# The first five pairs of sequences in turns of their own, and the last sum on TensorE, in an attention and mixture-of-experts kernel

## The reference, cut to what matters

```python
B, S, D = 16, 256, 128          # sequences, tokens, width; float32
qkv = x @ W_qkv + b_qkv         # q, k, v = split
attn = softmax(q @ k.T / sqrt(D))
x = layernorm(x + (attn @ v) @ W_out + b_out)
h = x + layer_norm(x, ln1_g, ln1_b) @ attn_w.T
t = layer_norm(h, ln2_g, ln2_b)
top_vals, top_idx = top_k(t @ gate_w.T, 2)       # 2 of 8 experts a token
rw = softmax(top_vals)
out = sum over experts e: comb[:, e] * (silu(t @ gate_proj[e].T) * (t @ up_proj[e].T)) @ down_proj[e].T
x = layernorm(h + out)          # INTER = 512
```

## Time and profile before

| | |
|---|---|
| median of 3 runs | 402.53 us (399.04 to 403.39) |
| profiled execution | 403.65 us |
| its span, first to last instruction | 401.8 us |
| PE busy | 312.1 us, 78% |
| DVE busy | 271.3 us, 68% |
| ACT busy | 241.3 us, 60% |
| POOL busy | 202.1 us, 50% |
| mean granted clock of PE | 0.878 |

### The profile page before, as it was taken

One profiled execution on the slowest core, in us unless ns is written; L12 is line 12 of the kernel. 1 busy time (PEld: TensorE's weight loads), 2 busy tenths in 40 slices (PEclk: granted clock), 3 DMA queues, 4 the chain that ended last, 5 costly groups with the idle time before them and its releaser, 6 DMA issues.

```text
span 401.8 us, 8647 instructions
## 1 busy us (share of the span) xinstructions
PE 312.1 (78%) x1972; PEld 267.2 (66%) x1972; DVE 271.3 (68%) x1079; ACT 241.3 (60%) x559; POOL 202.1 (50%) x251
## 2 busy tenths in 40 slices
PE   5645767776899999999999989989999999960000
PEld 4533556564778788888878878778898989850000
DVE  3353465667688688696878887877676766626990
ACT  3243543444668766866777677668777787731551
POOL 0001015565635585475568668588444442336980
PEclk9665575969899999999999999999999999995555
DMA  8234281201231131121112111223211111006851
GB/s 268 87 111 130 81 291 44 62 30 48 67 113 36 41 88 43 34 69 48 42 47 63 49 54 56 56 87 104 62 48 46 41 45 37 14 12 198 233 158 39
DMA packets 31967, 31.96 MB, mean 80 GB/s; under 512 B 4769, under 2 KB 27557, under 8 KB 31920
## 3 DMA queue, kind: packets, MB, share of 16 engines
q1 hardware_dynamic: 23248, 20.78, 18.3%
q0 software_dynamic: 4320, 8.53, 6.5%
q10 hardware_dynamic: 4352, 2.10, 1.7%
HBM read 20.16 MB, written 11.68 MB: 79 GB/s over the span
## 4 chain that ended last, share of the span: by engine, by line
PE 61%; DVE 13%; issue 11%; POOL 6%; ACT 5%; DMA 2%; ACTq 0%; SPq 0%; POOLq 0%; DVEq 0%
PE bank L514 15%; PE bank L467 7%; PE bank L469 7%; PE bank L468 7%; PE bank L500 7%; POOL expert_rows L1115 4%; PE bank L424 4%; PE bank L408 3%; PE bank L386 2%; PE bank L522 2%; PE bank L387 2%; PE bank L415 2%; PE bank L400 2%; DVE xs L1083 2%; DVE hid L1010 1%
## 5 line engine op out<-in xcount | busy, mean ns | idle before, releaser
L1124 POOL DMA_INDIRECT moe_rows<-ysb,xrow x71 | 70.6, 994 | 93.1 <-ACT ysb L661 85.8
L514 PE MATMUL bank<-wd,hidT 128*128 x568 | 76.4, 278 | 4.9 <-ACT t L668 4.1
L514 PEld LDWEIGHTS bank<-wd,hidT 128*128 128x128 f32 x568 | 69.0, 192 | 7.7 <-issue 7.6
L1115 POOL DMA_INDIRECT expert_rows<-rows,place x64 | 62.3, 974 | 22.4 <-issue 16.2
L467 PE MATMUL bank<-w_hi,t_hi 128*128 x142 | 62.6, 441 | 4.4 <-DVE hid L1010 4.3
L469 PE MATMUL bank<-w_hi,t_lo 128*128 x142 | 56.2, 396 | 0.0
L468 PE MATMUL bank<-w_lo,t_hi 128*128 x142 | 55.9, 394 | 0.0
L674 ACT ACTIVATE th<-bank 128x512 f32<-128x512 f32 x71 | 42.5, 599 | 14.3 <-PE bank L469 14.3
L1010 DVE SCALAR_TENSOR_TENSOR hid<-th,bank 128x512 f32<-128x512 f32 x71 | 48.3, 680 | 3.6 <-ACT th L674 3.4
L1014 DVE TENSOR_TENSOR hid<-hid,bank 128x512 f32<-128x512 f32 x71 | 48.8, 687 | 2.4
L687 ACT ACTIVATE hidT<-bank 128x512 f32<-128x512 f32 x71 | 42.5, 599 | 10.8 <-PE bank L500 10.8
(11 more groups left out here) (153 smaller groups left out, 599.6 us busy)
## 6 DMA issues: line engine op xcount, KB each, us to landing
xrow<-expert_rows SPq DMA_DIRECT2D x71, 66.0 KB, 1.9
w_raw<-weights SPq DMA_DIRECT2D x16, 256.0 KB, 2.7
w_raw<-moe_rows SPq DMA_DIRECT2D x16, 256.0 KB, 3.6
xT<-xt SPq DMA_DIRECT2D x8, 256.0 KB, 3.3
wd<-weights SPq DMA_DIRECT2D x4, 512.0 KB, 6.5
out<-xs ACTq DMA_DIRECT2D x16, 128.0 KB, 3.1
xs<-x SPq DMA_DIRECT2D x3, 512.0 KB, 5.0
moe_rows<-ysb,xrow POOLq DMA_INDIRECT x71, 2.3
```

Of the source, the lines that this page charges most:

```text
L514: last = mm(ps_y, hidT[i % 2][:, c * P:(c + 1) * P], wd[:, bass.ds(w + c * P, P)], start=(c == 0), stop=(c == NC - 1))
L1115: G.indirect_dma_start(out=expert_rows[:, :], out_offset=bass.IndirectOffsetOnAxis(ap=place[:, i, k:k + 1], axis=0), in_=rows[:, i, k, :], ...
L1124: G.indirect_dma_start(out=moe_rows[:, :], out_offset=bass.IndirectOffsetOnAxis(ap=xrow[i % XR][:, C_DST:C_DST + 1].bitcast(I32), axis=0), ...
```

## The change

The first five pairs (`FILL`) no longer go by the step counter. They go in five turns, and a turn n holds both sequences of pair n side by side: on two sets of banks (1, 3, 5 and 0, 2, 4, by `side(b)`) and two buffers each of `qT`, `kT` and `probT`. A turn also holds the later places of the pairs before it. The step counter goes on from `STEADY` = 40 as before for pairs 5 to 7 and the tail of pairs 2 to 4, with pairs four steps later (`- CHUNKS // 2` in `at`) and tiles seven steps later (`TILE_FROM` 42 for 35). In `finish`, DVE's and POOL's additions are replaced by three products with the identity on PE, which add up in PSUM over all 8 banks (`ps_z`). The w_lo pieces are made by POOL, 5, 7 and 4 of them in turns 0, 1 and 2, and their loads are issued by SP as early as the buffers allow. Scores and context no longer share a bank; values and context do.

```diff
@@ orders @@
-TILE_FROM = 35
+FILL = 5
+STEADY = CHUNKS * FILL
+TILE_FROM = STEADY + 2
+        PIECES = [(0, 5), (5, 12), (12, 16), (16, 16), (16, 16)]
         def at(q, r):
-            g, left = divmod(q - r, CHUNKS)
+            g, left = divmod(q - r - CHUNKS // 2, CHUNKS)
@@ banks @@
+        side = lambda b: 1 if b % 2 and b < 2 * FILL else 0
+        in_qp, in_s, in_vo = [banks[1], banks[0]], [banks[3], banks[2]], [banks[5], banks[4]]
+        in_a = lambda b: in_nr if b % 2 else banks[6] if b // 2 < FILL - 2 else banks[5]
+        ps_z = lambda b: banks[b % 8][:, 0:NT * D].rearrange("p (t d) -> p t d", t=NT)
@@ PE @@
             def qk(b):
-                if b >= 1:
-                    pe.wait_ge(sm["pT_sb"], b)
+                if b >= 2:
+                    pe.wait_ge(sm["pT_sb"], b - 1 if b < 2 * FILL else b)
             def values(b):
-                if b >= 1:
-                    pe.wait_ge(sm["v_sb"], b)
+                if b >= 2:
+                    pe.wait_ge(sm["y_done"], NT * (b - 1 if b < 2 * FILL else b))
             def scores(b):
-                if b >= 1:
-                    pe.wait_ge(sm["y_done"], NT * b)
+                if b >= 2:
+                    pe.wait_ge(sm["prob_done"], NT * (b - 1 if b < 2 * FILL else b))
+            for n in range(1, FILL):
+                qk(2 * n)
+                qk(2 * n + 1)
+                if n >= 3:
+                    rank(n - 3)
+                if n >= 2:
+                    turn_n1(n - 2)
+                scores(2 * n)
+                scores(2 * n + 1)
+                if n >= 2:
+                    attn_w(2 * (n - 2))
+                    attn_w(2 * (n - 2) + 1)
+                context(2 * n - 2)
+                context(2 * n - 1)
+                turn_prob(2 * n)
+                turn_prob(2 * n + 1)
+                values(2 * n)
+                values(2 * n + 1)
+            for b in range(B):
+                if b >= 8:
+                    pe.wait_ge(sm["o_done"], NT * (b - 7))
+                pe.wait_ge(y_in[b % RING], turn(b))
+                mm(ps_z(b), ident, xs[:, b, :, :], start=True, stop=False)
+                mm(ps_z(b), ident, yin[b % RING][:, :, 0, :], start=False, stop=False)
+                mm(ps_z(b), ident, yin[b % RING][:, :, 1, :], start=False, stop=True).then_inc(sm["z_done"], 1)
@@ ACT, a turn: what is new against the places of a pair @@
+                query_key(2 * n)
+                query_key(2 * n + 1)
+                ...
+                for i in range(third[0], third[1]):
+                    cast(i)
+                softmax(2 * n)
+                softmax(2 * n + 1)
+                ...
+                for j in range(GT if n < FILL - 1 else NT):
+                    x1(n - 1, j)
@@ DVE @@
-                i = piece(q)
-                if i is not None:
-                    dve.wait_ge(sm["whi_done"], i + 1)
-                    V.tensor_tensor(w_lo[:, :, cs], w_raw[i % NWR][:, :, :], w_hi[:, :, cs].bitcast(F32),
-                                    ALU.subtract).then_inc(sm["wlo_done"], 1)
             def finish(s, live):
                 if live(0):
-                    dve.wait_ge(sm["z0_done"], s + 1)
-                    V.tensor_tensor(xs[:, s, :, :], xs[:, s, :, :], yin[s % RING][:, :, 1, :], ALU.add
-                                    ).then_inc(sm["z_done"], 1)
                     dve.wait_ge(sm["z_done"], s + 1)
-                        V.bn_stats(st3[:, t, :], xs[:, s, t, :]).then_inc(sm["st3_done"], 1)
+                        V.bn_stats(st3[:, t, :], ps_z(s)[:, t, :]).then_inc(sm["st3_done"], 1)
@@ POOL @@
+            def split(i):
+                pool.wait_ge(sm["whi_done"], i + 1)
+                G.tensor_tensor(w_lo[:, :, cs], w_raw[i % NWR][:, :, :], w_hi[:, :, cs].bitcast(F32),
+                                ALU.subtract).then_inc(sm["wlo_done"], 1)
+            for n in range(1, FILL):
+                lo, hi = PIECES[n]
+                for i in range(lo, lo + (hi - lo) * 2 // 3):
+                    split(i)
+                if n >= 3:
+                    send_rows(n - 3, (0, 1, 2, 3))
+                if n >= 2:
+                    second_root(n - 2)
+                first_root(n - 1)
+                for i in range(lo + (hi - lo) * 2 // 3, hi):
+                    split(i)
+                if n >= 3:
+                    send_rows(n - 3, (4, 5, 6, 7))
             def finish(s, live):
-                    G.tensor_tensor(xs[:, s, :, :], xs[:, s, :, :], yin[s % RING][:, :, 0, :], ALU.add
-                                    ).then_inc(sm["z0_done"], 1)
```

More of the change, by code:

```diff
@@ L275, in turn, with second @@
             return per * (i // n + 1)
[L278 to L282, removed]
+        PIECES = [(0, 5), (5, 12), (12, 16), (16, 16), (16, 16)]
         def at(q, r):
-            g, left = divmod(q - r, CHUNKS)
+            g, left = divmod(q - r - CHUNKS // 2, CHUNKS)
             return g if left == 0 and 0 <= g < GROUPS else None
+        def second(q, r):
+            g = at(q, r)
+            return g if g is not None and g >= FILL else None
         def tile(q, stage):
@@ L544, in front @@
                     context(2 * g)
+                g = second(q, 4)
+                if g is not None:
                     qk(2 * g + 1)
@@ L1054, in late @@
                     plan_tiles(g)
[L1055 to L1066 removed]
+            largest(0)
+            largest(1)
             dve.wait_ge(sm["dst_in"], 16)
@@ L1074, in _ @@
                           ).then_inc(sm["fill_ready"], 2)
-            for q in range(6, ALL):
+            dve.wait_ge(sm["gate_ps"], 1)
+            V.tensor_copy(wa[:, D + E:D + 2 * E], banks[6][:, D:D + E]).then_inc(sm["wa_ready"], 1)
+            for n in range(1, FILL):
+                if n >= 3:
+                    places(n - 3)
+                largest(2 * n)
+                largest(2 * n + 1)
+                if n >= 2:
+                    hidden(2 * (n - 2))
+                    hidden(2 * (n - 2) + 1)
+                    second_variance(n - 2)
+                residual(2 * n - 2)
+                residual(2 * n - 1)
+                variances(n - 1)
+                if n >= 2:
+                    logits(n - 2)
+                    choose(n - 2)
+                x1_scale(n - 1)
+                if n == FILL - 1:
+                    plan_tiles(1)
+            places(FILL - 3)
+            for q in range(STEADY, ALL):
                 early(q)
@@ new lines, in send_rows @@
+            def send_rows(g, which):
+                if which[0] == 0:
+                    pool.wait_ge(sm["dest_ready"], 1)
+                    pool.wait_ge(sm["c_shift_done"], g + 1)
+                    pool.wait_ge(sm["cr_done"], g + 1)
+                    pool.wait_ge(sm["dup_done"], g + 1)
+                    pool.wait_ge(sm["place_done"], g + 1)
+                    pool.wait_ge(sm["wts_done"], 2 * g + 2)
+                for j in which:
+                    send(g, GT * g + j // TOPK, j % TOPK)
```

270 lines of the change are left out of this document (155 added, 115 removed).

## The result

| | before | after |
|---|---|---|
| median | 402.62 us (399.04 to 403.39, 4 runs) | 390.43 us (390.14 to 390.5, 4 runs) |
| profiled execution, its span | 403.65, 401.8 us | 390.5, 388.7 us |
| first tile's tanh | 110.1 us | 100.38 us |
| first to last tile's tanh | 242.95 us | 240.76 us |
| last tanh to the end of the span | 48.75 us | 47.56 us |

The ratio is 0.9713, 95% interval 0.9655 to 0.9771: faster by 2.9%, 12 us, where 28 were forecast. By the last three lines of the table, which split the spans of the two traces, the tile part gave 2.2 us (forecast 3.5) and the last part 1.2 (1.5). The first part gave 9.7 where 23 were forecast. That is 13.1 us in all, and of the 14.9 that are missing all but 1.6 lie before the first tile's tanh.

A forecast was written before the change was run, and what follows sets the result against it. Before the first tile a chain through four engines, one sequence in flight, was taken as the bound; after it, PE bounds the tiles. 403.65 - 23 - 3.5 - 1.5 = 375.7, given as 375 us; range 366 to 391.

The forecast's parts named there:

- term 1: First part, up to the first tile's tanh: 87 us instead of 110.1, 23 us earlier.
- Turn 2, "15": Second full turn, scores to scores: a 13.3 us loop plus about 2 us for half at the lower clock.
- The way to the first tile, "24": Turn 4's scores to first tanh: last send 17 us in, 2.4 to landing, load 2, remaining steps 3.
- at 1.27 it hides: First part: w_lo pieces on POOL, 1.27 us each, 16 of them 20 us over three turns, cost no time.
- The rival made of it: Turns 1 and 2: 11 POOL pieces each stop a DVE step for 1 us; 386 us, chance 0.06.
- Term 2: Tile part, first to last tanh: attention is 3 tiles further at the first tile; 3.5 us less.
- Term 3: Last part: sums move to PE, two cold sequences, then 1.4 us each; 1.5 us less.
- 1: First part: the turns stay at 1.2 GHz, first tanh at 98, 11 later; 386 us, chance 0.11.
- rival 2: Last part: PE never warms because a load is late each time; 391 us, chance 0.07.
- 5: First part: POOL's subtraction is dear, over 4.4 us a piece, so slower than before; chance 0.03.
- 3: Turns 1 and 2: POOL's pieces block DVE's steps, 1 us each; 386 us, chance 0.06.
- rival 4: First part: waits in order chain the turns at 20 us, so the fill gains little; 390 us, chance 0.07.

The follow-up runs named there:

- e1: Changed kernel, but POOL's last third of a turn's w_lo pieces waits until DVE's short operations are done; 410.55 us, ratio to before 0.9423.
- e3: Changed kernel, but ACT makes the next turn's qT and kT and the gap's exponential ahead of x1; 414.33 us, ratio to before 0.9493.
- e2: Changed kernel with the w_lo pieces back on DVE, in three groups a turn; 419.14 us, ratio to before 0.9618.
- e9: Changed kernel with powers before most pieces, late pieces waiting, ACT reordered, token-row products before the last part's first load, two pieces moved to turn 2; 403.64 us.
- e6: Changed kernel, but in turn 4 POOL sends all of pair 1's rows ahead of the two powers; 419.23 us, ratio to before 0.9539.
- e7: Changed kernel, but the last part's token-row products of the first eight sequences precede the first wait for a load; 415.36 us, ratio to before 0.9446.
- after_third: The changed kernel, unedited, run again beside the third set of experiments; 421.47 us, ratio to before 0.9624.

## Why the prediction was half right

**The step that failed** is term 1, the length of the turns and of the way to the first tile. It put at nothing the waits behind other work in the in-order lists of POOL, ACT and PE, and it said that POOL's pieces hide. The runs showed DVE's short operations standing still beside the pieces (e1), `turn_n1` standing behind the plan's `base` (e3), and contexts and query products ahead of the gate (read from the trace): turns of 17.0 and 19.5 us for 12 and 15, and 29.6 us to the first tile for 24.

**Direction and order of the terms: right.** The first part is where the time came from, and the chain of one sequence at a time was what bounded it.

**Term 1: wrong by 13.4 us**, first tanh at 100.38 for 87. In its steps:
- *Turn 0, "21":* 18.45, 2.5 us better.
- *Turn 1, "12":* 17.0. The step summed up what ACT has to do and held POOL to fit since its pieces' total is small. In its list pieces 7 and 8, which wait for casts, stand ahead of the power: 3.2 us, read from the trace. And DVE's short operations stood still beside the pieces behind it: 3.3 us, which e1 shows. The two make 6.5 where 5.0 are too much, so the first is not worth its full 3.2; no kernel took this wait away alone. In e1, where it stands, the turn is 1.8 us over the forecast, and in e2 and e9, where both are gone, it is 12.9 and 11.8 us.
- *Turn 2, "15":* 19.5. Of the 4.5 us too much, 2.1 are the same standstill (e1: 2.7 us for the turn), and some 2.2 are `turn_n1` behind `base` (e3: 3.5 us for the turn, clock included). The step had counted "the next qT and kT, 0.75" behind x1 and had not asked what PE does ahead of the scores.
- *Turn 3, "15":* 15.8. Here `base` cost 1.6 (e3), and other parts of the turn were shorter than counted.
- *The way to the first tile, "24":* 29.6. The 17 us to the last send were right (16.6), landing and load were 2 us too short, and "tn, transpose, t, split and the gate product, 3" had left out that contexts and query products stand ahead of the gate on PE. This part was not tried by itself: e6 changed what stands before it, and gained 1.0 us there.

In e9, which takes the causes in the turns away together and moves two pieces as well, the turns have the forecast's lengths or less. So the lengths of the turns as PE's, DVE's and ACT's work sets them were about right, and what was wrong is that nothing was counted for waits in order on POOL and ACT. With some luck: the forecast had half of a turn at the lower clock, and e9's turns had 0.90 to 0.97 granted.

**The weight pieces: price right, "at 1.27 it hides" wrong.** They took 1.264 us at the median. They hid in POOL's time, not in the time of those behind and beside them. The rule quoted from the Trainium skill, "SBUF — State Buffer" (Who interferes with whom), described what the trace then showed: `sd`, `lift` and `ratio` have two inputs in SBUF and ended with POOL's piece, while the row maximum, which reads a PSUM bank, took the same 0.69 us beside pieces (at 19.62, 20.48 and 37.56) as without one (39.27). The rival made of it, 11 us, was twice too dear, as five operations were caught and not eleven; but as a part of the sum, 5.4 us, it would have been the largest single correction inside the turns. I gave it 0.06 and the forecast itself nothing of it.

**Term 2: nearly right**, 2.2 us for 3.5. The pace of the tiles without attention was unchanged.

**Term 3: nearly right**, 1.2 for 1.5, by its own steps: two sequences at the lower clock, then 1.42 us each with their waits for loads where 1.4 was said. It left out that PE stands idle for 5.96 us ahead of them, and that is where e7 found 3.7 us.

**Rivals.** 1 and 2 fell: the granted clock was 0.76 to 0.93 in the turns and 1.00 in the last part from 359 us on. 5 fell with the price. 3 and 4 each held in part and at once: waits in order on ACT and POOL made turn 2 19.5 us, near rival 4's 20, but turns 1 and 3 not. The sum came out at rival 4's 390 without being its case. The stated range, 366 to 391, holds 390.43 by luck: its upper end is the price of rival 2, which did not happen. Treating the rivals as other worlds, each with its small chance, hid that parts of two of them were the likeliest case.

## What to carry to other kernels

A step's length is not the sum of one engine's work nor the largest such sum: for each wait that closes a loop, list what stands ahead of the awaited instruction on its own engine, and what that in turn waits for; three such lists (POOL's power, ACT's exponential, PE's gate) hold 8 to 10 of the 13 us here by the traces, of which ACT's alone was tried by itself. Work moved to an idle engine should be put behind what others wait for on that engine, and away from short operations of DVE with two SBUF inputs, or it costs more than it did where it was. And what makes the first tile earlier must not make the steps behind it later: compare first to last tile as well, in an execution near the median, and the granted clock beside each stretch.

## What the runs showed of the hardware that I had not expected

- Tiny operations of DVE with two inputs in SBUF took 1.18 to 1.30 us instead of 0.15 to 0.17 beside a subtraction of 128x512 on POOL (1.27 us). The other way round, the power on POOL took 2.01 us instead of 1.64 in e2, where it began beside DVE's pieces (27.02 us, DVE's pieces from 26.84).
- The same kernel took 390 us in the first pair of runs and 420 us on the two chips of the experiments. The extra time isn't spread: the last 30 tiles take the same (85.2 us from the 41st tanh to the last in the first trace, 85.0 in after_third), but from the first to the 41st tanh it is 155.5 against 179.4 us, and from turn 4's scores to the first tanh 29.6 against 36.2. That is the time in which POOL sends the tokens' rows (the last of these sends is issued at 253.4 and at 280.1 us), and engines waited there for what by the trace was done. DVE, after_third first, and then the same two operations of the first trace, back to back:

```profile
97.74 0.29 DVE L966 BATCH_NORM_STATS2 st<-rows 128x6 f32<-128x128 f32 x1 [1.44 <-DVE rows L959]
99.14 0.29 DVE L966 BATCH_NORM_STATS2 st<-rows 128x6 f32<-128x128 f32 x1 [1.11 <-remote]
```

```profile
92.01 0.48 DVE L966 BATCH_NORM_STATS2 st<-rows 128x6 f32<-128x128 f32 x2
```

  Why an engine waits over a microsecond for its own finished operation there, and only in these sets, stays open; no kernel was made for it. The kernel before is 34 to 37 us longer there, the changed one 30 to 31, so comparisons are made inside a set.
